# Relational layer rows: node tiles outside, bases inside, with the base products of a tile set between the rows of the tile before it

## The reference, cut to what matters

```python
def _L2_gnn_ref(x, bases, w_comp, h_bias, norm, src, dst, etype):
    n_nodes = x.shape[0]                                  # 625 nodes, 512 features
    weight = jnp.einsum('rb,bio->rio', w_comp, bases)     # 32 relations from 8 bases
    h_rel = jnp.einsum('ni,rio->rno', x, weight)
    msg = h_rel[etype, src] * norm                        # 20000 edges
    out = jax.ops.segment_sum(msg, dst, num_segments=n_nodes)
    return out + h_bias

x = x + _L2_gnn_ref(_layernorm(x), L2_gnn_bases, L2_gnn_w_comp, L2_gnn_h_bias, edge_weight1, src, dst, edge_type_32)
```

## Time and profile before

| what | us |
|---|---|
| median of the 3 runs shown | 5803.34 |
| lowest and highest of them | 5794.79, 5803.74 |
| the profiled execution, its own time | 5798.81 |
| its span, first to last instruction | 5797.0 |
| mean granted TensorE clock in it | 0.947 of full |

### The profile page before, as it was taken

One profiled execution on the slowest core, in us unless ns is written; L12 is line 12 of the kernel. 1 busy time (PEld: TensorE's weight loads), 2 busy tenths in 40 slices (PEclk: granted clock), 3 DMA queues, 4 the chain that ended last, 5 costly groups with the idle time before them and its releaser, 6 DMA issues. The chain is left out here.

```text
span 5797.0 us, 266500 instructions
## 1 busy us (share of the span) xinstructions
PE 4898.6 (85%) x108902; PEld 3080.6 (53%) x109528; DVE 2840.1 (49%) x11510; ACT 1431.7 (25%) x4741; POOL 653.7 (11%) x1090
## 2 busy tenths in 40 slices
PE   8999686894899897888888888888888888777788
PEld 6643343332466444666666666666666666544444
DVE  4501344211455574555555555555555555574543
ACT  0000000001233252333333333333333333242222
POOL 0000382000365110000000000000000000021000
PEclk9899897997999998999999999999999999988877
DMA  0010111166643751000000000000000000001100
GB/s 11 15 37 8 33 42 34 51 133 188 212 120 100 260 183 44 10 12 10 12 10 10 12 10 11 11 10 12 10 10 12 10 12 10 6 26 40 62 22 9
DMA packets 158173, 265.03 MB, mean 46 GB/s; under 512 B 54102, under 2 KB 89052, under 8 KB 153745
## 3 DMA queue, kind: packets, MB, share of 16 engines
q1 hardware_dynamic: 92140, 161.15, 8.3%
q0 software_dynamic: 65952, 102.82, 7.1%
HBM read 178.38 MB, written 85.14 MB: 45 GB/s over the span
## 5 line engine op out<-in xcount | busy, mean ns | idle before, releaser
L1487 PE MATMUL bank<-lstm_w,step_h_parts 128*32 128x128 f16 x87360 | 1451.7, 220 | 243.3 <-issue 243.3
L1487 PEld LDWEIGHTS bank<-lstm_w,step_h_parts 128*32 128x32 f16 x87360 | 1236.5, 97 | 614.7 <-issue 350.3
L1558 DVE TRANSPOSE_TENSOR_REDUCE step_summed<-bank 128x4 f32 (+1 forms) x2500 | 792.3, 317 | 1084.6 <-PE bank L1487 913.2
L1482 PE MATMUL bank<-step_xg,step_rows 128*128 (+1 forms) x1876 | 617.0, 384 | 177.2 <-issue 157.7
L1455 ACT ACTIVATE step_act_out<-step_summed,lstm_inv_scale 128x4 f32<-128x4 f32 x625 | 185.8, 297 | 1726.8 <-DVE step_summed L1558 1726.8
L1443 POOL COPY xnT<-step_state 128x4 f32 (+1 forms) x625 | 117.4, 188 | 2759.0 <-DVE step_state L1583 2759.0
L1108 PE MATMUL bank<-sum_parts,sum_hot 125*125 125x512 f16 x1600 | 347.9, 381 | 6.8 <-DVE sum_parts L1067 6.8
L1108 PEld LDWEIGHTS bank<-sum_parts,sum_hot 125*125 125x125 f16 x1600 | 219.3, 137 | 135.8 <-DVE sum_parts L1067 7.6
L1358 PE MATMUL bank<-xg_w,xnT 128*125 128x512 f32 x640 | 277.0, 596 | 6.9 <-DMA xg_w<-in_c_w_ih 6.9
L538 POOL DMA_INDIRECT gcn_rows<-gcn_h_rows,gcn_idx x160 | 202.2, 1264 | 703.0 <-issue 702.7
L1482 PEld LDWEIGHTS bank<-step_xg,step_rows 128*128 128x128 bf16 x2500 | 142.6, 97 | 167.9 <-issue 130.0
(11 more groups left out here) (373 smaller groups left out, 6439.1 us busy)
## 6 DMA issues: line engine op xcount, KB each, us to landing
rel_h<-rel_h_sb SPq DMA_DIRECT2D x39, 1024.0 KB, 4.3
lstm_xg<-cnt POOLq DMA_DIRECT2D x80, 375.0 KB
step_xg<-lstm_xg SPq DMA_DIRECT2D x375, 80.0 KB, 2.4
xg_w<-in_c_w_ih SPq DMA_DIRECT2D x16, 1024.0 KB
lstm_w<-in_c_w_hh SPq DMA_DIRECT2D x16, 1024.0 KB, 9.3
rel_z<-rel_z_sb POOLq DMA_DIRECT2D x8, 1250.0 KB, 23.0
rel_zg<-rel_z POOLq DMA_DIRECT2D x8, 1248.0 KB, 14.5
cheb_w<-in_L_gnn_weight SPq DMA_DIRECT2D x8, 1024.0 KB
```

The lines of the kernel that those rows point to most:

```text
L1482: return nc.tensor.matmul(bank[:], rows[:, p, :], xg[:, at, :], start=True, stop=stop)
L1487: last = nc.tensor.matmul(bank[32 * q:32 * q + 32, 128 * s:128 * s + 128], h_parts[:, c, :], w[:, s, c, q, a, 128 * p:128 * p + 128], star ...
L1558: nc.vector.tensor_reduce(summed[:, 4 * p:4 * p + 4], bank[:, bass.ds(s * 128, 128)].rearrange("p (b r) -> p b r", r=32), X_AXIS, ALU.add, ...
```

## The change

The loops of the first phase change places: tiles of 128 nodes (the last has 113) are outside and the 8 bases inside, so all 8 bases are loaded at once into `rel_bases`, now 8 buffers, with no wait between the loads, and ahead of most of the small tables. TensorE's program becomes `multiply(0)`, `multiply(1)`, `combine(0)`, `multiply(2)`, `combine(1)` and so on: 32 matmuls that make the z of one tile, then 32 that make the rows of the tile before it. PSUM's eight banks are used in turn over both kinds of product (`z_turn`, `h_turn`), even turns copied by VectorE, odd ones by ScalarE. `rel_z_sb` becomes four buffers of one product each. Every product of z is stored alone (256 KB) and, when the eight bases of a tile are stored, the tile's eight groups are loaded as one transfer (`z_groups`) that fills all 128 partitions. `rel_zg` holds two tiles in place of all groups. The stores and loads of z move from GpSimd's queue to SP's, where they stand in one program order with the stores of h.

```diff
-    z_dram = nc.dram_tensor("rel_z", (NB, N, D), F32, kind="Internal").ap()
+    z_dram = nc.dram_tensor("rel_z", (NG + 1, NB, GROUP, D), F32, kind="Internal").ap()
+    def z_turn(m, b):
+        return b if m == 0 else NB + (m - 1) * (NB + 8 * Q) + b
+    def h_turn(g, q):
+        m = g // 8
+        return (NB + m * (NB + 8 * Q) + (NB if m < LAST else 0)) + (g % 8) * Q + q
-        wb = sb("rel_bases", [128, 2, KC, D], F32)
-        z = sb("rel_z_sb", [R, 2, NT, D], F32)
-        zg = sb("rel_zg", [128, NG, D], F32)
+        wb = sb("rel_bases", [128, NB, KC, D], F32)
+        z = sb("rel_z_sb", [128, 4, D], F32)
+        zg = sb("rel_zg", [128, 2, 8, D], F32)
...
         def _(sp):
+            def z_rows(m, b):
+                j = z_turn(m, b)
+                sp.wait_ge(kept_a if j % 2 else kept_v, j // 2 + 1)
+                full = len(groups_of(m)) * GROUP
+                sp.dma_start(z_dram[8 * m:8 * m + len(groups_of(m)), b], z[0:full, b % 4, :]
+                             ).then_inc(z_stored[b % 4], 16)
+                if m == LAST:
+                    sp.dma_start(z_dram[NG, b, 0:1, :], z[full:full + 1, b % 4, :]).then_inc(z_stored[b % 4], 16)
+            def z_groups(m):
+                k = len(groups_of(m))
+                for i in range(4):
+                    sp.wait_ge(z_stored[i], 16 * (NB // 4) * (m + 1 + (1 if m == LAST else 0)))
+                sp.dma_start(zg[:, m % 2, 0:k, :], z_dram[8 * m:8 * m + k].rearrange("g b i d -> (b i) g d")
+                             ).then_inc(z_loaded[m], 16)
...
+            for m in range(NT):
+                for b in range(NB):
+                    z_rows(m, b)
+                z_groups(m)
+                if m >= 1:
+                    for g in groups_of(m - 1):
+                        h_rows(g)
+            for g in groups_of(LAST):
+                h_rows(g)
...
-        @block.gpsimd
-        def _(pool):
-            for b in range(NB):
-                pool.wait_ge(z_kept_a, 2 * (b + 1))
-                pool.wait_ge(z_kept_v, 3 * (b + 1))
-                pool.dma_start(z_dram[b].rearrange("(j p) d -> p j d", p=R), z[:, b % 2]).then_inc(z_stored[b % 2], 16)
-                pool.wait_ge(z_stored[b % 2], 16 * (b // 2 + 1))
-                pool.dma_start(zg[b * GROUP:(b + 1) * GROUP, :, :],
...
         @block.vector
+            for m in range(NT):
+                for b in range(0, NB, 2):
+                    keep_z(m, b)
+                    if m == 0:
+                        look(b)
+                        look(b + 1)
...
         @block.tensor
+            def bank_free(j):
+                if j >= BANKS:
+                    pe.wait_ge(kept_a if j % 2 else kept_v, (j - BANKS) // 2 + 1)
...
+            multiply(0)
+            for m in range(1, NT):
+                multiply(m)
+                combine(m - 1)
+            combine(LAST)
```

More of the change, by code:

```diff
@@ L796, in relational, with rows_of, groups_of @@
         relational_sum(nc, ctx, B)
+def rows_of(m):
+    return min(128, N - 128 * m)
+def groups_of(m):
+    return range(8 * m, min(8 * m + 8, N // GROUP))
 def relational_rows(nc, ctx, B):
@@ L806, in relational_rows @@
     Q = GROUP // QN
+    LAST = NT - 1
+    BANKS = 8
     def sb(name, shape, dt):
@@ L873, in _ @@
         @block.vector
         def _(dve):
[L875 to L890, removed]
@@ L891, in _, with keep_z, keep_h @@
-            for g in range(NG):
+            def keep_z(m, b):
+                j = z_turn(m, b)
+                z_free(dve, m, b)
+                dve.wait_ge(filled, j + 1)
+                nc.vector.tensor_copy(z[0:rows_of(m), b % 4, :], B.bank[j % BANKS][0:rows_of(m), :]
+                                      ).then_inc(kept_v, 1)
+            def keep_h(g, q):
+                j = h_turn(g, q)
                 if g >= 3:
                     dve.wait_ge(h_stored[g % 3], 16 * (g // 3))
[L894 to L897, removed]
@@ L901, in _ @@
+            for g in groups_of(LAST):
+                for q in range(0, Q, 2):
+                    keep_h(g, q)
+            dve.wait_ge(filled, LAST_TURN + 1)
+            nc.vector.tensor_copy(h_last[:], B.bank[LAST_TURN % BANKS][0:NR, :]).then_inc(kept_v, 1)
         @block.scalar
         def _(act):
[L903 to L908, removed]
@@ L909, in _, with keep_z, keep_h @@
-            for g in range(NG):
+            def keep_z(m, b):
+                j = z_turn(m, b)
+                z_free(act, m, b)
+                act.wait_ge(filled, j + 1)
+                nc.scalar.copy(z[0:rows_of(m), b % 4, :], B.bank[j % BANKS][0:rows_of(m), :]).then_inc(kept_a, 1)
+            def keep_h(g, q):
+                j = h_turn(g, q)
                 if g >= 3:
                     act.wait_ge(h_stored[g % 3], 16 * (g // 3))
[L912 to L915, removed]
+                act.wait_ge(filled, j + 1)
+                nc.scalar.copy(ho[:, g % 3, q, :], B.bank[j % BANKS][:]).then_inc(kept_a, 1)
@@ L917, in _ @@
+            for m in range(NT):
+                for b in range(1, NB, 2):
+                    keep_z(m, b)
+                if m >= 1:
+                    for g in groups_of(m - 1):
+                        for q in range(1, Q, 2):
+                            keep_h(g, q)
+            for g in groups_of(LAST):
+                for q in range(1, Q, 2):
+                    keep_h(g, q)
         @block.tensor
         def _(pe):
[L919 to L923, removed]
[L925 to L933 removed]
@@ new lines, in combine @@
+            def combine(m):
+                pe.wait_ge(mix_ready, 1)
+                pe.wait_ge(z_loaded[m], 32 if m == LAST else 16)
+                for g in groups_of(m):
+                    for q in range(Q):
+                        j = h_turn(g, q)
+                        bank_free(j)
+                        nc.tensor.matmul(B.bank[j % BANKS][:],
+                                         mix[:, q * QN:(q + 1) * QN, :].rearrange("p i r -> p (i r)"),
+                                         zg[:, m % 2, g % 8, :], start=True, stop=True).then_inc(filled, 1)
@@ L953 @@
+            multiply(0)
[3 more added lines that the diff above has]
+            combine(LAST)
+            bank_free(LAST_TURN)
+            nc.tensor.matmul(B.bank[LAST_TURN % BANKS][0:NR, :], compT[:], z_last[:], start=True, stop=True
+                             ).then_inc(filled, 1)
 BUFS = 4
```

106 lines of the change are left out of this document (56 added, 50 removed).

## The result

The changed kernel takes 5703.57 us (median of four runs) where the kernel before takes 5801.06; the ratio is 0.9831, with a 95% interval of 0.9816 to 0.9845. That is 97.5 us less, the forecast was 5700. One of the four runs, 7176.51 us at a mean granted clock of 0.642, is a disturbed one, as is one of the four of the experiment with the wait for all (13713.63 us): the medians of all runs given here hold them (without it the changed kernel's is 5700.23), the ratios leave them out. The profiled execution took 5706.91 us, its span is 5705.1.

A forecast was written before the change was run, and what follows sets the result against it. TensorE bounds the stage outside its five holes; 5.3 + (2.47 + 3.27 + 2.79 + 77.90) + 8.9 = 100.6 us, less 2 for late banks, 98.6, takes 5798.81 to 5700 us; range 5690 to 5730.

The forecast's parts named there:

- TensorE's work: Matmuls of the stage: 632 records at 0.428 us, 270.5 us, the same before and after; nothing gained or lost.
- The start: First base issued first in SP's queue, not behind ten small loads, landing 5.6 us after issue: gain 5.3 us.
- Waits for bases: TensorE's waits for base loads in the first phase go, as all eight are issued in a row: 2.47 + 3.27 us.
- for z buffers: TensorE's wait for a free z buffer goes, 2.79 us; VectorE is late by 3 us, TensorE not at all.
- The hole: TensorE's idle stretch between base products and rows: z's store and load fit under 27.4 us of other work, gaining 77.90 us.
- What is late next: At the sixth group of tiles 1 to 4, TensorE may wait for a bank: 0.5 us each time, 2 us in all.
- Its upper bound: Bank waits if z's load runs at 106 GB/s: 11.8 us each time, 47 us in all; chance in full 0.06.
- the late banks: PSUM banks freed late at a tile's sixth group because stores of h stand behind z's load: 2 us lost in all.
- Clock: TensorE restarts at the lower clock after holes cost 11.9 us; one restart of 3.0 stays, gain 8.9 us.
- Waits on TensorE: Each row product waits for its own bank and signals by itself, 156 times: put at 0, 5 us if each cost 30 ns.
- The end: From TensorE's last product to the next stage: 5.2 us, as before.

The follow-up runs named there:

- the experiment with the wait for all: Changed kernel with all five tiles of z before all rows, the first group waiting for the loads of all tiles: 5721.75 us, ratio 0.9855.
- the old succession without the wait for all: Changed kernel with all five tiles of z before all rows, each group waiting only for its own tile's load: 5700.91 us, ratio 0.9823.
- the narrow loads: Changed kernel with each tile's load of z cut into eight, each writing 16 partitions: 5755.35 us, ratio 0.9911.
- the two variants without the late banks: Changed kernel with z's load issued behind the stores of h, 5700.06 us; the same with the first base also in four pieces, 5698.5 us.
- one cut at partition 112: Kernel before with each base's store of z cut into two stores of 112 and 13 partitions: 5748.72 us, ratio 0.9913.

## Why the prediction was right

The time, the sign and the mechanism held. Step by step, with the profile of the changed kernel:

- *TensorE's work, 270.5 us, unchanged:* right. Blocks of 64 records stand every 27.47 us, 0.429 us a record.
- *The start, 5.3 us:* too large by 1.5. The first base landed 7.1 us after its issue, not 5.6 (1134.45 to 1141.53). The base was issued first as forecast; the landing time was carried over from the kernel before, and why it is longer here stays open.
- *Waits for bases, 5.7 us, and for z buffers, 2.8:* right, none is left. VectorE waited 1.9 us once for a z buffer (3 forecast), TensorE not at all. SP needed 10.71 us to issue six bases, which moved the first store of z to 1155.08, and that too fitted.
- *The hole, 77.90 us:* right, and right for the reason given in the sentence "so the hole goes whichever it is": the old succession without the wait for all has none either, and the narrow loads bring none back between a tile's z and its rows.
- *What is late next, 2 us:* right in place (the sixth group, ended by a copy that waited for a store of h) and in size (1.9 us). The chain to it was longer than I worked out, 5.0 us and 9.3 in place of 3.9 and 7.2, and it used up the 2 us in hand. That the size came out is in part luck: the 0.5 us a time was an allowance, for the working had left those 2 us over. The stores of z had half of the engines busy: a share of 0.51 and 178 GB/s.
- *Its upper bound, 47 us:* with the narrow loads the stage grew by 48 us against the changed kernel, of which 41.1 are waits (47 expected). The lower clock behind them, which the bound had left out, adds 10.2; the late banks that were there before (1.9 us) and an earlier start come off.
- *Clock, 8.9 us:* right. One restart is left, 2.9 us (57.76 us to the first row against 54.9 for 128 records at 0.429).
- *Waits on TensorE at 0:* right; in the two variants without the late banks the blocks of rows too run at 27.47 us for 64 records, with a wait before every product.
- *The end, 5.2 us:* 4.7 (1418.67 to 1423.39).

The measured sum is 96.9 us for the stage against 98.6: 1.5 less at the start, some 0.8 because a record took 0.429 us and not 0.428, and 0.5 back at the end. The profiled execution, against which the sum was made, came to 5706.91 us and not 5700, for outside the stage it took 5 us longer; the two other undisturbed runs (5700.23 and 5699.98) come nearer to the forecast than the sum itself warrants.

What the prediction did not see is how much of the gain can be had without the new order. It read the 0.31 and the 106 GB/s as reasons for the hole and priced the order alone. The runs show 52 us to be had from one cut at partition 112, 39 of them in the hole, and with the new transfers a wait for all of z costs 13 us and not 78. That the hole is gone with both is shown; what the new order would gain over the old one with wide loads as well isn't.

## What to carry to other kernels

When TensorE waits at the end of a phase for a line of transfers, look first at the DMA share and the rate in the windows while they run: a low share at a fair rate per engine, or a full share at a quarter of the rate (here 0.31 at 126 GB/s, and 1.04 at 106), was here a matter of the transfer's shape, and the first could be mended where it stood. A change of order then hides what is left, and it is the dependency (wait for a tile, not for all) and other work between a tile's z and its rows that hide it, not how finely the kinds of work alternate. In a queue that holds both, put the transfer that has 27 us of time behind the ones that free buffers now.

## What the runs showed of the hardware that I had not expected

While stores of h stood in line behind a load of z, the DMA engines moved 409 GB/s at a share of 1.05; the forecast had taken 365 from the base loads. Large loads in a row held up the queue that issued them: six of 1 MB took SP 10.71 us to issue, some 1.8 us each, where a lone issue takes 0.37. Holes of 12.9 to 13.4 us cost TensorE another 1.7 to 3.1 us of lower clock when work came back, up to what the hole of 78 us cost (3.2).
